# One engine's one-hot moved to another, an engine program without drains, and a re-ordered group of a graph layer

## The reference, cut to what matters

```python
xn = _layernorm(x)
msgs = edge_weight[:, None] * xn[src]                      # 53125 edges, sorted by dst
agg = segment_sum(msgs, dst, 3125) @ gnn_W.T + gnn_b
Q, K = elu(xn @ Wq) + 1, elu(xn @ Wk) + 1                  # 8 heads
msg = attention of Q with K's and V's sums                 # linear: KV = K^T V once
msg = _layernorm(msg @ Wm, g1, b1)
h = relu(concat([xn, msg]) @ W1) @ W2                      # W1 512x512, W2 512x256
x = x + agg + xn + _layernorm(h, g2, b2)
x = x + ffn(_layernorm(x))                                 # 16 experts, the best 2 of each token
```

## Time and profile before

| | |
|---|---|
| median of 3 runs | 1311.46 us (1310.92 to 1312.66) |
| profiled execution, its own time | 1313.73 us |
| its span, first to last instruction | 1311.6 us |
| mean granted TensorE clock | 0.940 |
| PE busy in the span | 1113.1 us (85%) |
| DVE, ACT, POOL busy | 801.9 us (61%), 679.3 us (52%), 606.2 us (46%) |

### The profile page before, as it was taken

How to read it: one execution, slowest core, us unless ns; L and a number is a source line. 1 busy time by engine, 2 the same in 40 slices (tenths; PEclk the granted TensorE clock), 3 DMA queues, 4 the chain that set the end, 5 groups by cost and what they waited for, 6 DMA issues and landing times.

```text
span 1311.6 us, 21107 instructions
## 1 busy us (share of the span) xinstructions
PE 1113.1 (85%) x6272; PEld 935.6 (71%) x6272; DVE 801.9 (61%) x1963; ACT 679.3 (52%) x1630; POOL 606.2 (46%) x625
## 2 busy tenths in 40 slices
PE   6797788988889888888888888972999999999990
PEld 5675676766667677676766766731899999999980
DVE  7874777868778786877868685777222222222226
ACT  4556696878778688887968885431011111111100
POOL 5846455565655656566565656001233333333320
PEclk9896798999999999999989998986999999999995
DMA  7213122222222222222222222025699999999958
GB/s 210 83 49 108 57 69 71 71 77 77 77 70 76 73 69 77 75 79 73 73 76 70 76 78 87 3 98 172 238 335 333 317 338 334 333 327 332 334 189 297
DMA packets 113486, 196.08 MB, mean 149 GB/s; under 512 B 13505, under 2 KB 61439, under 8 KB 113407
## 3 DMA queue, kind: packets, MB, share of 16 engines
q1 hardware_dynamic: 84073, 120.62, 27.4%
q0 software_dynamic: 26112, 71.34, 17.4%
q10 hardware_dynamic: 3222, 3.20, 0.7%
HBM read 177.12 MB, written 17.99 MB: 149 GB/s over the span
## 4 chain that ended last, share of the span: by engine, by line
PE 52%; DVE 17%; DVEq 8%; ACT 8%; issue 8%; another core or an unknown queue 3%; ACTq 2%; DMA 1%; SPq 0%; POOL 0%; POOLq 0%
PE psum L1061 18%; PE psum L1071 8%; PE psum L965 8%; PE psum L974 4%; DVE agg L1322 4%; PE psum L896 3%; ACT in_slot L414 3%; DVE agg L1328 2%; ACT first_use L428 2%; PE psum L886 2%; PE psum L905 1%; DVE agg L1684 1%; PE psum L853 1%; PE psum L1049 1%
## 5 line engine op out<-in xcount | busy, mean ns | idle before, releaser
L703 POOL DMA_INDIRECT arena<-y_rows,gather_i x416 | 432.9, 1041 | 323.9 <-PE psum L965 105.3
L965 PE MATMUL psum<-arena,hot 128*128 128x256 f32 x832 | 227.2, 402 | 30.2 <-issue 15.3
L1322 DVE TENSOR_TENSOR agg<-psum,agg 128x256 f32 x416 | 175.0, 421 | 63.7 <-PE psum L965 29.7
L636 ACT ACTIVATE arena<-psum 128x512 f32<-128x512 f32 x64 | 38.3, 598 | 327.8 <-issue 187.8
L965 PEld LDWEIGHTS psum<-arena,hot 128*128 128x128 f32 x832 | 155.7, 199 | 70.5 <-issue 48.5
L1061 PEld LDWEIGHTS psum<-arena 128*128 128x128 f32 x1536 | 179.7, 193 | 6.7 <-issue 4.7
L1061 PE MATMUL psum<-arena 128*128 128x128 f32 x1536 | 181.4, 277 | 2.0 <-DVE arena L1641 2.0
L1648 DVE TENSOR_TENSOR arena<-psum,arena 128x512 f32<-128x512 f32 x64 | 44.3, 692 | 215.3 <-PE psum L1061 215.3
L974 PE MATMUL psum<-arena,first_use 128*128 x624 | 156.7, 386 | 18.9 <-issue 9.7
L531 ACT ACTIVATE arena<-arena,listed 128x256 f32<-128x256 f32 x416 | 171.9, 498 | 1.3 <-DMA arena<-y_rows,gather_i 1.3
L719 POOL DMA_INDIRECT chosen_rows<-arena,back_at x64 | 63.4, 990 | 219.7 <-DVE arena L1655 215.0
(11 more groups left out here) (221 smaller groups left out, 1625.3 us busy)
## 6 DMA issues: line engine op xcount, KB each, us to landing
arena<-in_L_ffn_w_dram SPq DMA_DIRECT2D x144, 512.0 KB
xnT<-in_L_ffn_w_dram SPq DMA_DIRECT2D x48, 512.0 KB
arena<-y_rows,gather_i POOLq DMA_INDIRECT x416
arena<-chosen_rows SPq DMA_DIRECT2D x4, 1280.0 KB, 9.9
y_rows<-w ACTq DMA_DIRECT2D x6, 512.0 KB, 2.9
agg<-in_x_dram SPq DMA_DIRECT2D x4, 640.0 KB, 6.7
n_rows<-arena SPq DMA_DIRECT2D x4, 640.0 KB
out_dram<-agg SPq DMA_DIRECT2D x4, 640.0 KB
```

The source lines that it names most:

```text
L703: pool.indirect_dma_start(rows[h][:, t, :], None, y_rows, bass.IndirectOffsetOnAxis(ap=gather_i[h][:, t:t + 1], axis=0)).then_inc(gathered ...
L965: pe.matmul(bank_of(g, t // 2)[:, (t % 2) * C:(t % 2 + 1) * C], hot[:, (g * GT + t) % HOTS, :], rows[h][:, t, :], start=True, stop=True).t ...
L1322: dve.tensor_tensor(own, bank_of(g, t // 2)[:, (t % 2) * C:(t % 2 + 1) * C], own, ALU.add).then_inc(evicted, 1)
```

## The change

1. **The slots' one-hot moves from ACT to DVE.** ACT's `slot_hot` is gone (8 Abs, a drain and a Relu for a chunk, four chunks a group). DVE's new `mark_slots` makes it with one bf16 comparison; `in_slot` is stored in pairs, so PE loads every second bf16 value as its weights.
2. **The cross rows' one-hots have 24 places** in place of 16; the wait inside the group is gone, one wait for the group before stays.
3. **DVE's functions lose their drains.** Where the order itself doesn't separate two dependent operations, `dve.drain()` is written out. In groups 1 to 12 a new table sets the order, group 0 keeps an order near to the old one (`beside_first`), with drains.
4. **The order in groups 1 to 12.** The prefix stands at the group's start (PE step 1, DVE step 0) and not at step 20 and 17; the bins are marked and counted a group earlier; the list is finished at the group's end. W1's first two products stand behind step 19 together, the third behind 20 and the last behind 23. The query moves from step 25 to 28, the attention from 49 to 47, the reorders from 33, 40, 46, 54 to 20, 26, 32, 33. The load of the cross rows' tile numbers into PE's registers moves from the group's start to row 15.

```diff
-            def slot_hot(g, k):
-                act.wait_ge(places_ready, g + 1)
-                if g * CHUNKS + k >= 2:
-                    act.wait_ge(reordered, g * CHUNKS + k - 1)
-                for c in range(CH):
-                    act.activation(in_slot[k % 2][:, c, :], iota[:, :], ACT.Abs, bias=place_f[:, k * CH + c:k * CH + c + 1])
-                act.drain()
-                act.activation(in_slot[k % 2][:, :, :], in_slot[k % 2][:, :, :], ACT.Relu, scale=-1.0, bias=1.0).then_inc(slot_hot_ready, 1)
...
             def cross_hot(g, b):
-                k = g * (CROSS // BATCH) + b
                 act.wait_ge(picks_kept, g + 1)
-                if b == 2:
-                    act.wait_ge(met, g * STEPS + GT + BATCH)
-                elif g >= 1:
-                    act.wait_ge(met, (g - 1) * STEPS + GT + (b + 2) * BATCH)
+                if g >= 1:
+                    act.wait_ge(met, (g - 1) * STEPS + GT + (b + 1) * BATCH)
...
+            def mark_slots(g, k):
+                if g * CHUNKS + k >= 2:
+                    dve.wait_ge(reordered, g * CHUNKS + k - 1)
+                whole = [P, CH // 2, P, 2]
+                two = place_b[:, 1, k * CH:(k + 1) * CH].rearrange("p (a b) -> p a b", b=2)
+                dve.tensor_tensor(in_slot[k % 2][:, :, :, :], two.unsqueeze(2).to_broadcast(whole), slot_no[:, :, :].unsqueeze(1).to_broadcast(whole),
+                                  ALU.is_equal).then_inc(slot_hot_ready, 1)
...
             def make_record(g, k):
-                dve.drain()
                 if g * CHUNKS + k >= 2:
                     dve.wait_ge(reordered, g * CHUNKS + k - 1)
...
-                if step == (21 if g == 0 else 19):
+                if step == 19:
                     hidden(g, 0)
-                if step == 20 and sorts:
-                    prefix(g + 2)
-                if step == (23 if g == 0 else 21):
                     hidden(g, 1)
-                if step == 22:
+                if step == 20:
+                    if sorts:
+                        reorder(g + 2, 0)
                     hidden(g, 2)
-                if step == 25 and more:
-                    query(g + 1)
-                if step == 29:
+                if step == 23:
                     hidden(g, 3)
...
+                    if t == 15:
+                        pe.wait_ge(list_ready, g + 1)
+                        _, row_of = nc.values_load_multi_w_load_instructions(
```

More of the change, by code:

```diff
@@ L908, in down, with beside_first @@
                     last.then_inc(d_down, 1)
+            def beside_first(step):
+                if step == 3:
+                    attend(0)
+                if step == 4:
+                    turn_list(1)
+                if step == 9:
+                    turn_tok(0, d_msg, d_msgT)
+                if step == 12:
+                    merge(0)
+                if step == 13:
+                    pick_list(1)
+                if step == 19:
+                    turn_tok(0, d_n1, d_n1T)
+                if step == 20:
+                    prefix(2)
+                if step == 21:
+                    hidden(0, 0)
+                if step == 22:
+                    hidden(0, 2)
+                if step == 23:
+                    hidden(0, 1)
+                if step == 25:
+                    query(1)
+                if step == 29:
+                    hidden(0, 3)
+                if step == 34:
+                    down(0, 0)
+                if step == 35:
+                    down(0, 1)
+                if step == 49:
+                    attend(1)
+                if step in (33, 40, 46, 54):
+                    reorder(2, (33, 40, 46, 54).index(step))
@@ L948, in beside @@
-                if step == 54 and sorts:
-                    reorder(g + 2, 3)
+                if step == 26:
+                    if sorts:
+                        reorder(g + 2, 1)
+                if step == 28:
+                    if more:
+                        query(g + 1)
+                if step == 32:
+                    down(g, 0)
+                    if sorts:
+                        reorder(g + 2, 2)
+                if step == 33:
+                    if sorts:
+                        reorder(g + 2, 3)
+                    if len(pair_of(g)) == 2:
+                        down(g, 1)
@@ L1483, in add_up @@
+                if step == 51:
+                    if more:
+                        message_shares(g + 1)
+                    if sorts:
+                        drop_whole(g + 2)
+                if step == 55:
+                    if sorts:
+                        mark_starts(g + 2)
+                    if more:
+                        message(g + 1, 0)
+                    if more:
+                        message(g + 1, 1)
             def add_up(g, its_bin):
```

494 lines of the change are left out of this document (309 added, 185 removed).

## The result

The changed kernel takes 1291.99 us (median of 4 runs, 1289.63 to 1294.94) beside 1311.19 us for the one before (4 runs, 1310.85 to 1312.66): ratio 0.9853, 95% interval 0.9831 to 0.9875. It is 19.2 us faster, where 47 were forecast (1264 us). The sign is right and the time lies inside the range, but less than half of the gain came.

A forecast was written before the change was run, and what follows sets the result against it. PE was taken as nearest to a bound, 49.6 of 57.1 us busy a group. Savings of 3.85 us a group, 38.5 in ten groups, and 9.1 elsewhere made 47.6 us: 1264 us, range 1224 to 1296.

The forecast's parts named there:

- The hold's own cost on PE: PE's completions reach nobody for some microseconds while W1's products run; some 3 us a group, kept unchanged.
- Clock, 3.5 us: PE in groups 1 to 10: fewer idle stretches, fewer clock falls; 0.35 us a group, between 0 and 0.7.
- Cross rows' one-hots: PE's cross rows: the last eight no longer wait for the first eight of their group; 1.3 us a group saved.
- Evictions: PE's wait for evictions goes, as DVE no longer stands at the prefix amid the rows; 1.1 us a group saved.
- Relu and query: PE's wait at the query for ACT's relu goes, slot one-hots having left ACT; 0.6 us a group saved.
- Message: PE's wait at the transpose for DVE's message goes, its operations standing a group earlier; 0.5 us a group saved.
- Register load: PE's sequencer at row 15: hidden behind queued rows and a transpose; cost 0, at most 1.6 us a group.
- W1's products in one stretch: W1's products on PE: their number is the same, so no gain was counted.
- Slots on DVE: Slot comparisons on DVE: 0.70 us each, 2.8 us a group more busy time, hidden behind PE.
- Strided weights: PE's reorder products loading every second value as weights: taken as 0, bounds 0 to 3 us a group.
- the hold goes: Rival: PE's late completions vanish or no longer hurt; groups of 49.3 us, 1224 us in all; chance 0.17.
- Waits move: Rival: evictions', relu's and message's waits return elsewhere; 26 us saved, 1286 us, or 1302 with the load; chance 0.18.

The follow-up runs named there:

- sp_reads: Changed kernel, each gather of groups 2 to 12 replaced by a plain 128 KB read issued by SP at the same gates; 1217.39 us, ratio 0.9303.
- before_no_gathers: Kernel before the change, POOL's gathers of groups 2 to 12 left out; 1254.3 us, ratio 0.9583.
- even2: Changed kernel, gather gates from group 2 on at even shares of group time, by step times of the run without gathers; 1247.32 us, ratio 0.9449.
- spread_no_gathers: Changed kernel, W1's products back at steps 19, 21, 22 and 29, gathers of groups 2 to 12 left out; 1262.79 us, ratio 0.9579.
- before_even: Kernel before the change, gather gates from group 2 on at even shares of its own group's time; 1308.41 us, ratio 0.9988.

## Why the prediction was off

*The step that failed* is this sentence: "The hold's own cost on PE (...) I keep unchanged". I took it for a property of W1's products. It belongs to POOL's gathers, whose gates are counted in PE's steps, so every move of work between steps moves it. For groups 1 to 10 the windows give what the gathers cost: before, 571.0 - 515.1 = 55.9 us; after, 553.6 - 488.2 = 65.4 us, of which the traffic is next to nothing (0.3 us in the changed kernel, by sp_reads). So the "some 3 us a group" were 5.6, and they became 6.5. That is 9.5 us of the 21.1 missing in these groups; 3.5 more are the clock's term and 8.1 the others', both below. By the medians the gathers cost 54.5 us before and 72 to 79 after, so 10 us is the lower end. The hold itself is even shorter than it was (4.9 us beside 6.9, as means); it costs more, as far as the trace shows, because PE has only cross rows left, runs out of banks, stands 3 us and then works at the lower clock for 6.8 us. That last chain is read from the trace, and no run separates the clock's part from the wait's.

*Clock, 3.5 us:* didn't come, 0.93 after 0.97. Without the gathers both kernels have it in full (1.00 and 0.99), the one before with all its idle stretches of up to 1.5 us. So the falls came with the gathers and not with the stretches that I wanted to remove.

*The other terms* made 35 us in ten groups. Without gathers the windows show 515.1 - 488.2 = 26.9. Groups 2 to 8 give 3.6 each, where the sum has 3.5. Group 1 is 3.9 us longer instead of 3.5 shorter (53.4 beside 49.5): 3.3 of it is one wait of PE at the prefix, for group 1's step 1 needs a list that DVE finishes at the end of group 0; I had counted group 1 like the rest. Cross rows' one-hots: right (12.6 and now none; 13 forecast). Evictions: 6.1 of the 10.8 were their own, the rest the hold's. Relu and query: no such wait is in before_no_gathers, so all of it was the hold's. Message: more than forecast, 11.9 beside 4.8. Against them stand the pick's new wait, 1.2 us a group, which is in no term (I had followed the moved transpose only to DVE), and the register load.

*Register load:* put at 0 with 1.6 as its upper end, because a row and a transpose were to cover it. It starts only when the last of these, the transposes, do, and they cover 0.6 of its 1.6 us: it costs 1.0 us in every group without gathers and in even2, and 7.8 us in the ten groups of the changed kernel.

*W1's products in one stretch* I gave no gain. By spread_no_gathers it is 4.0 us a group within the new orders. So the agreement in the middle groups is luck. In the two windows of one group the idle time of PE falls by 1.8 us (4.2 to 2.4), the waits that went less the two that came, and its busy time by another 1.8 (47.5 to 45.6), which I had taken as fixed. With the stretch undone the busy time is back, so that half belongs to a change that had no term.

*Slots on DVE:* 685 ns each, forecast 700. But DVE's busy time didn't grow by 2.8 us a group, only by 0.2. The drains did matter: without one an operation starts before the one ahead of it has ended (0.68 us at 410.88, the next at 411.49). The durations of DVE's instructions in the ten groups do add up to 24.8 us more than before (510.7 beside 485.9), but busy time counts an overlap once. The record's operation has 1.1 us of idle time ahead of 52 of it instead of 4.7. This is also the answer to the rule on drains that I quoted: without one the 0.09 us are gone here, and more.

*Strided weights:* 0 was right, eight products take 0.96 us beside 0.97. *Keys' stage and group 0:* 3.1 us together, 4.3 forecast; *groups 11 and 12:* 3.5 us, 4.8 forecast.

*The rivals:* "the hold goes" would have been 1224; without holds it is 0.925 to 0.930 of 1311, 1213 to 1220 us, so that rival named the right unknown and priced it well, in part by luck: it took PE's busy time as 48.3 us a group, and 45.6 were left. "Waits move" gave 1286 and is nearest to what happened, by another mechanism. DVE never became the bound.

What stays open: why gathers under way delay PE's completions, and whose completions they delay besides. Those of the transfers themselves do arrive meanwhile. Of DVE and ACT the traces can't tell: of the updates of DVE in the ten groups 118 of 680 have no record within 1 us of their instruction's end, and none of 682 without the gathers; in group 5's hold the eviction that ended at 405.53 us has none. The Trainium skill, "DMA: Bandwidth & Descriptors", section "SWDGE vs HWDGE vs iDMA", says that GpSimd writes such descriptors into rings in SBUF, a path that hardware descriptors never touch. sp_reads agrees in so far as it has no hold; no run here shows the rings as the reason.

## What to carry to other kernels

When an engine waits for a semaphore whose work is long done on the profile ("remote"), look at what every other engine is doing in those microseconds before you treat the wait as fixed: here four kernels, without gathers, with plain reads, with other work on POOL, and ungated, settled it. Pace a stream of indirect DMAs by time and not by steps whose length a change can alter; work the paces out again after each reordering, from a trace without the disturbance (even2 had it and before_even had not). And price a change with the disturbance taken out of both kernels: 3% was there, of which the measurement showed half.

## What the runs showed of the hardware

- Completions of PE come late while indirect DMAs of POOL pile up, at 1.25 us from one to the next: about 1 us in rows of four, 5 in rows of eight, 7 in rows of twelve; with rows of 32, twenty waits of DVE at its evictions end "remote", after 8.4 us in the mean and 18.4 at most. None with drained gathers 3.5 us apart, none with 128 KB reads issued by SP, none with arithmetic on POOL.
- The hold at a row's end lasts until the last gather has landed, 2.6 us after that gather began (ten groups of ten in the changed kernel).
- A drain issued with a gather lasts 3.0 us on POOL, until the gather has landed, so 3.5 us a gather in place of 1.25.
- 3.1 us of idle time on PE were followed by 6.8 us at 1.2 GHz; a row's product of 256 columns has 631 ns in the mean there and 379 ns at the full clock.
- Some 320 subtractions of 128x256 floats on POOL made DVE's busy time 5% longer (442.9 to 465.6 us).
- A load of 24 registers on PE's sequencer takes 1.6 us; where it starts together with the last queued products (0.66 us of transposes), 1.0 us of it shows as idle time of PE.
